# A diffusion step's sums packed into fewer gaps of a dense pipeline, with the boundary product and the next step moved later

## The chip, the cores and the metric

The kernel runs on one core of one Trainium2 chip. The metric is the device time of one execution in microseconds (us); the profile is that of one execution on the same core.

## The reference, cut to what matters

The program is a graph network of four blocks on 50,000 nodes of 256 features with 12,500 edges. What matters here is the last block. It ends in a linear diffusion of six steps (gamma is 0):

```python
x = silu(h @ W_in.T + b_in)
out = term = x
for i in range(1, 7):
    msg = term[src]                                   # gather over edges
    term = (segment_sum(msg, dst) * inv_deg) / i      # per node
    out = out + term
x = layernorm(h + out @ W_out.T + b_out)
```

Nodes that no edge points to have a term of zero: for them the whole network is a chain of dense products and layer norms, row by row.

## The kernel before, in words

The edges are sorted by target and cut into T = 100 tiles of 128 rows of a table. The six steps are computed in reverse (Horner) form, each one reading one of two tables in HBM (`h`, `h2`) and writing the other. One tile of one step, here called **one sum**, is: GpSimd gathers 128 rows by index into `i_messages` (L616, an indirect DMA whose descriptors GpSimd makes), SyncE loads a 128x128 matrix of equal keys `i_equal` (L2726), TensorE multiplies the two into one of four PSUM banks (L2801), VectorE scales it and adds the accumulator into `i_y` (L2838), SyncE stores `i_y` to the other table (L2731).

A step ends with its **boundary**: sums of nodes whose edges cross tiles. SyncE waits until all stores of the step have landed and reads the tiles' end rows back into `i_ends` (L2736), TensorE multiplies them by a triangular matrix (L2797), VectorE adds (L2832), GpSimd scatters the result into the table (`put_bound`, L2769). Only when that scatter has landed may GpSimd gather for the next step.

Beside it, in the same stage (`diffuse`), runs the dense network of the nodes without edges, class `Dense`, 160 units of 256 rows in a software pipeline of 165 **turns**. Each engine's program is written out by hand, in order. A turn has four places called **gaps** at which the engine's part of the diffusion is put in, so there are 660 gaps, 110 for each step. In a turn VectorE runs L709, L711, L714, gap, L866, L907, gap, L889, L891, L881, L882, gap, L873, L875, L900, gap. TensorE runs project (L810), gap, transposes (L674), gap, output product (L828), gap, hidden product (L819), gap. GpSimd runs two gaps, then one power operation `powers` (L926) that serves three layer norms of different units, and two gaps more. `powers` waits for L891 and L882 of the same turn of VectorE. Its result is read by L900 in the same turn of VectorE and by ScalarE (L851, L859), whose L851 must be done before L709 of the next turn.

The function `places` says which sum stands in which gap. Before, sum t of a step that begins at gap g0 stands in gap g0 + t, the boundary in g0 + 105, and the next step begins at g0 + 110. TensorE takes a sum in its gap, VectorE adds it one gap later, SyncE stores it two gaps later. GpSimd makes gathers one gap later, for eight sums ahead, at most two in a gap:

```python
if t == T:
    put_bound(s)
upto_q = min((s + 1) * T if t < T else STEPS * T, s * T + t + AHEAD + 1)
...
for k in range(2):
    if fetched < upto_q:
        get(fetched)
        fetched += 1
```

So at the gap behind the boundary GpSimd scatters and from there makes the next step's first nine gathers, two in a gap. GpSimd's gaps with a number 4k and 4k + 1 lie ahead of `powers` of turn k, 4k + 2 and 4k + 3 behind it. When `diffuse` is done, the stage `output` reads the last table.

Of the kernel before, what the change touches and what calls it, by code (L numbers as in the profile page):

```python
# [16 lines left out]
STEPS = 6  # L17
# [2656 lines left out]

def places(T, gaps):

    at = {}
    for s in range(STEPS):
        g0, g1 = gaps * s // STEPS, gaps * (s + 1) // STEPS
        for t in range(T):  # L2680
            at[g0 + t * (g1 - g0 - 9) // T] = (s, t)
        at[g1 - 5] = (s, T)
    assert len(at) == STEPS * (T + 1)
    return at


def diffuse(net):
# [8 lines left out]
    with Stage(nc) as st:  # L2696
        dn = Dense(net, st.ctx, "n", net.early, Dense.all_units(net) - net.early)
        dn.banks(*st.ps("n_bank", 4))
        banks = st.ps("i_bank", 4)
        acc = st.sb("i_acc", [P, T, D])  # L2700
        M = st.sb("i_messages", [P, D], n=NM)
        EQ = st.sb("i_equal", [P, P], n=NM)
        Y = st.sb("i_y", [P, D], n=NY)
        EF = st.sb("i_ends", [T, 2, D])
        B = st.sb("i_bound", [T, D])
        scale = st.sb("i_scale", [P, STEPS, T])
        acc_in, got, eq_in, stored = st.sem("i_acc_loaded", T // CHUNK), st.sem("i_gathered", NM), st.sem("i_eq_loaded", NM), st.sem("i_stored", NY)
        scale_ready, summed, added, ends_in, scattered, copied = (
            st.sem(f"i_{n}") for n in ("scale_ready", "summed", "added", "ends_loaded", "scattered", "copied"))
        assert T % NM == 0 and T % NY == 0 and T % CHUNK == 0  # L2710
        TURNS = dn.units + 5
        GAPS = TURNS * dn.PIECES
        at = places(T, GAPS)
        nth = lambda s, t: s * (T + 1) + t + 1
        block = st.ctx.enter_context(nc.Block())

        def summed_before(eng, q):
            if q >= NM:
                eng.wait_ge(summed, nth((q - NM) // T, (q - NM) % T))

        @block.sync
        def _(sp):
            def load_eq(q):
                if q < STEPS * T:
                    summed_before(sp, q)
                    sp.dma_start(EQ[q % NM][:], net.eq_tab[q % T, :, :]).then_inc(eq_in[q % NM], 16)  # L2726

            def store(s, t):
                q = s * T + t
                sp.wait_ge(added, nth(s, t))  # L2730
                sp.dma_start(tabs[(s + 1) % 2][t * P:(t + 1) * P, :], Y[q % NY][:]).then_inc(stored[q % NY], 16)  # L2731

            def load_ends(s):
                for b in range(NY):
                    sp.wait_ge(stored[b], 16 * (T // NY) * (s + 1))
                sp.dma_start(EF[:], tabs[(s + 1) % 2][0:R, :].rearrange("(t p) d -> t p d", p=P)[:, 0:2, :]).then_inc(ends_in, 16)  # L2736
            n = itertools.count()

            def gap():
                i = next(n)  # L2740
                if i - 2 in at and at[i - 2][1] < T:
                    store(*at[i - 2])
                    if at[i - 2][1] == T - 1:
                        load_ends(at[i - 2][0])
                if i in at and at[i][1] < T:
                    load_eq(at[i][0] * T + at[i][1] + AHEAD)
            for u in range(2):
                dn.load(sp, 0, u)
            for q in range(AHEAD):
                load_eq(q)  # L2750
            for i in range(TURNS):
                dn.turn_sp(sp, i // 2, i % 2, gap)
            for u in range(2):
                sp.wait_ge(dn.stored[u], 16 * (dn.units // 2))

        @block.gpsimd
        def _(gp):
            def get(q):
                s, t = q // T, q % T
                summed_before(gp, q)  # L2760
                if s:
                    gp.wait_ge(scattered, 16 * s)
                if s == 1:
                    gp.wait_ge(copied, 64)
                gather(net, M[q % NM][:], tabs[s % 2], net.table_row[:, t:t + 1]).then_inc(got[q % NM], 16)

            def put_bound(s):
                gp.wait_ge(added, nth(s, T))
                nc.gpsimd.indirect_dma_start(tabs[(s + 1) % 2], bass.IndirectOffsetOnAxis(net.bound_row[:, 0:1], 0), B[:], None,  # L2769
                                             bounds_check=R - 1, oob_is_err=False).then_inc(scattered, 16)  # L2770
            n, fetched, upto_q = itertools.count(), 0, AHEAD

            def gap():
                nonlocal fetched, upto_q
                i = next(n)
                if i - 1 in at:
                    s, t = at[i - 1]
                    if t == T:
                        put_bound(s)
                    upto_q = min((s + 1) * T if t < T else STEPS * T, s * T + t + AHEAD + 1)  # L2780
# [4 lines that stand above are left out]
            for i in range(TURNS):  # L2785
                dn.turn_gp(gp, i // 2, i % 2, gap)
            gp.wait_ge(scattered, 16 * STEPS)

        @block.tensor
        def _(pe):  # L2790
            def total(s, t):
                q, r = s * T + t, nth(s, t) - 1
                if r >= 4:
                    pe.wait_ge(added, r - 3)
                if t == T:
                    pe.wait_ge(ends_in, 16 * (s + 1))
                    nc.tensor.matmul(banks[r % 4][0:T, 0:D], net.upper[:], EF[:, 0, :], start=True, stop=True).then_inc(summed, 1)  # L2797
                else:
                    pe.wait_ge(eq_in[q % NM], 16 * (q // NM + 1))
                    pe.wait_ge(got[q % NM], 16 * (q // NM + 1))  # L2800
                    nc.tensor.matmul(banks[r % 4][:, 0:D], EQ[q % NM][:], M[q % NM][:], start=True, stop=True).then_inc(summed, 1)  # L2801
            n = itertools.count()

            def gap():
                i = next(n)
                if i in at:
                    total(*at[i])
            for i in range(TURNS):
                dn.turn_pe(pe, i // 2, i % 2, gap)

        @block.scalar
        def _(act):
            for c in range(T // CHUNK):
                act.dma_start(acc[:, c * CHUNK:(c + 1) * CHUNK, :],
                              net.h[c * CHUNK * P:(c + 1) * CHUNK * P, :].rearrange("(t p) d -> p t d", p=P)).then_inc(acc_in[c], 16)
            for c in range(4):
                rows = slice(R + c * (R // 4), R + (c + 1) * (R // 4))
                act.dma_start(net.h2[rows, :], net.h[rows, :]).then_inc(copied, 16)
            for i in range(TURNS):
                dn.turn_act(act, i // 2, i % 2)  # L2820

        @block.vector
        def _(dve):
            V = nc.vector

            def add(s, t):
                q, r = s * T + t, nth(s, t) - 1
                dve.wait_ge(summed, r + 1)
                if t == T:
                    if s:  # L2830
                        dve.wait_ge(scattered, 16 * s)
                    V.tensor_tensor(B[:], banks[r % 4][0:T, 0:D], EF[:, 1, :], ALU.add).then_inc(added, 1)  # L2832
                else:
                    if s == 0 and t % CHUNK == 0:
                        dve.wait_ge(acc_in[t // CHUNK], 16)
                    if q >= NY:
                        dve.wait_ge(stored[q % NY], 16 * (q // NY))
                    V.scalar_tensor_tensor(Y[q % NY][:], banks[r % 4][:, 0:D], scale[:, s, t:t + 1], acc[:, t, :], ALU.mult, ALU.add).then_inc(added, 1)  # L2838
            n = itertools.count()

            def gap():
                i = next(n)
                if i - 1 in at:
                    add(*at[i - 1])
            for s in range(STEPS):
                V.tensor_scalar(scale[:, s, :], net.inv_deg[:], 1.0 / (STEPS - s), None, ALU.mult).then_inc(scale_ready, 1)
            dve.wait_ge(scale_ready, STEPS)
            for i in range(TURNS):
                dn.turn_dve(dve, i // 2, i % 2, gap)
# [218 lines left out]
```

## Time and profile before

| | |
|---|---|
| median of 3 runs | 3917.52 us (3917.25 to 3924.81) |
| the profiled execution | span 3924.5 us; its own time is taken as the 3924.81 us among the runs, so 0.3 us lie around the span |
| stage `diffuse` in the trace | about 2440 to 3725 us |
| TensorE over the span | 83% busy, mean granted clock 0.914 |
| VectorE, GpSimd, ScalarE | 72%, 53%, 48% busy |

Rows of the trace give the start in us from the start of the span, the duration in us, the engine and line, the operation, and in brackets how long the engine had been idle before and what released it. PEld is TensorE's weight load: each fp32 product has several, and in a saturated stretch they stand without holes. DVE is VectorE, POOL GpSimd, ACT ScalarE, PE TensorE.

### The profile page before, as it was taken

Reading aid. Unit: us, or ns where it says so; the run is one execution under the profiler, and the core shown is the slowest. Engines: PE = TensorE matmul, PEld = TensorE weight load, DVE = VectorE, ACT = ScalarE, POOL = GpSimd, SP = SyncE. Lnnn points to the kernel's source line nnn. Section 1 sums busy time; section 2 is a strip of 40 time slices with the busy share of each in tenths; the row PEclk is TensorE's granted clock in tenths of the full one; section 3 lists DMA queues with packets and bytes.
Section 4 is the critical chain, followed back from the end, with each engine's and each line's share of the span. In section 5 each row is a group of like instructions: output and inputs, shape, how many; then the busy total and the mean of one; then the engine's idle time right before and its main releaser. Section 6 shows DMA issues by size and latency. Waiting matters only on the chain. (4 is left out here: it accounts for less than half of the span.)

```text
span 3924.5 us, 56642 instructions
## 1 busy us (share of the span) xinstructions
PE 3261.1 (83%) x14868; PEld 2626.7 (67%) x14868; DVE 2815.4 (72%) x7890; ACT 1882.4 (48%) x5403; POOL 2087.1 (53%) x2120
## 2 busy tenths in 40 slices
PE   5999927688576899477999993599999999999865
PEld 4888715476454566245777772587878787888754
DVE  5676768698587466794666662598989898989733
ACT  3777705466333121142333331366666666666555
POOL 4767500475365666033333322476767676767667
PEclk8999958899799999657999996799999999999998
DMA  5788739443375333183333335886868686878765
GB/s 145 244 244 247 235 95 354 153 134 108 107 211 174 94 88 87 54 247 99 111 116 115 111 110 187 283 252 199 251 201 252 197 251 201 253 208 242 209 210 164
DMA packets 690467, 710.71 MB, mean 181 GB/s; under 512 B 73444, under 2 KB 644190, under 8 KB 689796
## 3 DMA queue, kind: packets, MB, share of 16 engines
q1 hardware_dynamic: 592204, 484.13, 39.8%
q0 software_dynamic: 68288, 181.26, 17.1%
q10 hardware_dynamic: 29660, 41.70, 3.2%
q8 instruction: 126, 2.06, 0.2%
q14 instruction: 189, 1.55, 0.1%
HBM read 427.77 MB, written 296.22 MB: 184 GB/s over the span
## 5 line engine op out<-in xcount | busy, mean ns | idle before, releaser
L616 POOL DMA_INDIRECT s_i_messages<-h,table_row x600 | 614.0, 1023 | 190.4 <-issue 158.3
L2801 PE MATMUL s_i_bank<-s_i_messages,s_i_equal 128*128 128x256 f32 x1200 | 362.5, 386 | 74.3 <-issue 36.6
L926 POOL TENSOR_TENSOR n_powers<-n_powers,neg_half 128x8 f32<-128x8 f32 (+3 forms) x164 | 268.5, 1637 | 229.9 <-DVE n_powers L891 149.4
L851 ACT ACTIVATE n_z<-gamma_bc,n_powers 128x256 f32<-128x256 f32 x320 | 174.8, 593 | 356.5 <-POOL n_powers L926 356.5
L810 PE MATMUL s_n_bank<-w,n_xt 128*128 128x256 f32 x1280 | 306.9, 383 | 22.6 <-DMA n_xt<-in_x_t 22.6
L828 PE MATMUL s_n_bank<-w_out,n_ht 128*128 128x256 f32 x1280 | 311.7, 387 | 5.6 <-ACT n_ht L838 5.3
L2838 DVE SCALAR_TENSOR_TENSOR s_i_y<-s_i_bank,s_i_scale,s_i_acc 128x256 f32<-128x256 f32 x600 | 285.2, 476 | 34.3 <-PE s_i_bank L2801 32.2
L819 PE MATMUL s_n_bank<-n_x3t,w_in 128*128 128x256 f32 x1280 | 303.2, 380 | 0.0
L2801 PEld LDWEIGHTS s_i_bank<-s_i_messages,s_i_equal 128*128 128x128 f32 x1200 | 219.3, 193 | 101.1 <-issue 42.2
L810 PEld LDWEIGHTS s_n_bank<-w,n_xt 128*128 128x128 f32 x1280 | 246.0, 192 | 58.0 <-DMA n_xt<-in_x_t 23.8
L828 PEld LDWEIGHTS s_n_bank<-w_out,n_ht 128*128 128x128 f32 x1280 | 247.3, 195 | 46.2 <-ACT n_ht L838 11.9
L819 PEld LDWEIGHTS s_n_bank<-n_x3t,w_in 128*128 128x128 f32 x1280 | 243.9, 191 | 33.4
L616 POOL DMA_INDIRECT s_a_x<-in_x,index x200 | 197.8, 989 | 97.4 <-issue 96.3
L2101 PE MATMUL s_e_ps_qv<-w_qv,s_e_xt 128*128 128x512 f32 x400 | 189.7, 597 | 0.0
L2116 ACT ACTIVATE s_e_xt<-s_e_ps_t 128x512 f32<-128x512 f32 x100 | 59.7, 597 | 264.3 <-PE s_e_ps_t L2091 264.3
L2405 POOL TENSOR_TENSOR s_g_small<-s_g_small,neg_half 128x2 f32<-128x2 f32 (+1 forms) x51 | 43.7, 857 | 243.2 <-DVE s_g_small L2648 243.2
L2640 DVE SCALAR_TENSOR_TENSOR s_g_y<-s_g_x,real,s_g_bank 128x512 f32<-128x512 f32 x50 | 37.3, 747 | 179.5 <-PE s_g_bank L2496 179.5
L682 ACT ACTIVATE n_squares<-n_u 128x256 f32<-128x256 f32 x320 | 130.2, 408 | 73.2 <-issue 62.5
L2536 ACT ACTIVATE s_g_h<-s_g_hidden,real 128x512 f32<-128x512 f32 x50 | 36.1, 722 | 251.0 <-DVE s_g_hidden L2595 175.8
L900 DVE TENSOR_SCALAR n_x<-n_z,n_small,n_powers 128x256 f32<-128x256 f32 x320 | 118.3, 412 | 50.9 <-POOL n_powers L926 37.2
L695 ACT ACTIVATE n_x3t<-s_n_bank 128x512 f32<-128x512 f32 x160 | 95.4, 596 | 108.6 <-PE s_n_bank L674 103.9
L859 ACT ACTIVATE n_w<-n_w,n_powers 128x256 f32<-128x256 f32 x320 | 142.8, 493 | 9.1 <-POOL n_powers L926 9.1
(444 smaller groups left out, 9169.7 us busy)
## 6 DMA issues: line engine op xcount, KB each, us to landing
h<-s_i_y SPq DMA_DIRECT2D x600, 128.0 KB, 3.9
n_xt<-in_x_t SPq DMA_DIRECT2D x160, 256.0 KB
out<-n_w SPq DMA_DIRECT2D x160, 256.0 KB
s_i_equal<-eq_tab SPq DMA_DIRECT2D x600, 64.0 KB
x<-s_x_rows SPq DMA_DIRECT2D x100, 256.0 KB
out<-s_a_hs SPq DMA_DIRECT2D x100, 128.0 KB
proj_dst<-s_a_hd SPq DMA_DIRECT2D x100, 128.0 KB
h<-s_h_rows SPq DMA_DIRECT2D x50, 256.0 KB, 4.1
```

The lines of the kernel that those rows point to most:

```text
L616: return net.nc.gpsimd.indirect_dma_start(out, None, table, bass.IndirectOffsetOnAxis(index, 0))
L682: sq = self.nc.scalar.activation(self.squares[0][:, g, :], self.U[u][:, g, :], ACT.Square, scale=self.D ** -0.5, accum_out=self.S[u][:, g: ...
L810: mm = self.nc.tensor.matmul(self.pr[:, g * self.D:(g + 1) * self.D], self.XT[u][:, c, g * P:(g + 1) * P], self.net.w12[:, c, :], start=c ...
L819: mm = self.nc.tensor.matmul(self.hd[:, 2 * m * P:2 * (m + 1) * P], self.net.w_in[:, c, m * P:(m + 1) * P], self.X3T[:, c, :], start=c == ...
L828: mm = self.nc.tensor.matmul(self.op[:, g * self.D:(g + 1) * self.D], self.HT[:, m, g * P:(g + 1) * P], self.net.w_out[:, m, :], start=m = ...
L851: sc = self.nc.scalar.activation(self.Z[u][:, g, :], self.net.bc["gamma"][:], ACT.Identity, bias=v[:, 8 + g:9 + g], scale=v[:, 10 + g:11 + g])
L859: nm = self.nc.scalar.activation(self.W[u][:, g, :], self.W[u][:, g, :], ACT.Copy, scale=v[:, 14 + g:15 + g])
L900: nm = self.nc.vector.tensor_scalar(self.X3[u][:, g, :], self.Z[u][:, g, :], s[:, 24 + 2 * g:25 + 2 * g], v[:, 12 + g:13 + g], ALU.subtrac ...
L926: self.nc.gpsimd.tensor_tensor(v[:, 8 + b0:8 + b1], v[:, b0:b1], self.net.neg_half[:, 0:b1 - b0], ALU.pow).then_inc(self.powered, 1)
L2101: mm = nc.tensor.matmul(qvs[b][:, :], XT[b][:, c, :], net.w_qv[:, c, :], start=c == 0, stop=c == C - 1)
L2801: nc.tensor.matmul(banks[r % 4][:, 0:D], EQ[q % NM][:], M[q % NM][:], start=True, stop=True).then_inc(summed, 1)
L2838: V.scalar_tensor_tensor(Y[q % NY][:], banks[r % 4][:, 0:D], scale[:, s, t:t + 1], acc[:, t, :], ALU.mult, ALU.add).then_inc(added, 1)
```

## The change

`places` is given two constants. The 100 sums of a step stand in its first 90 gaps, so every ninth gap from the first (g0, g0 + 9, ..., g0 + 81) holds two sums and the others one. The boundary stands in g0 + 99, and the gaps from g0 + 90 on hold no sum until the next step at g0 + 110. Since a gap may hold several sums, the table of places holds lists and each engine goes through the list. Counted from the last sum, the boundary comes ten gaps later in place of six, and the next step's first sum 21 gaps later in place of eleven.

```diff
 def places(T, gaps):
 
-    at = {}
+    FREE, BEHIND = 20, 9
+    at = {i: [] for i in range(-2, gaps + 2)}
     for s in range(STEPS):
         g0, g1 = gaps * s // STEPS, gaps * (s + 1) // STEPS
         for t in range(T):
-            at[g0 + t * (g1 - g0 - 9) // T] = (s, t)
-        at[g1 - 5] = (s, T)
-    assert len(at) == STEPS * (T + 1)
+            at[g0 + t * (g1 - g0 - FREE) // T].append((s, t))
+        at[g1 - FREE + BEHIND].append((s, T))
+    assert sum(len(v) for v in at.values()) == STEPS * (T + 1)
     return at
...
             def gap():      # SyncE
                 i = next(n)
-                if i - 2 in at and at[i - 2][1] < T:
-                    store(*at[i - 2])
-                    if at[i - 2][1] == T - 1:
-                        load_ends(at[i - 2][0])
-                if i in at and at[i][1] < T:
-                    load_eq(at[i][0] * T + at[i][1] + AHEAD)
+                for s, t in at[i - 2]:
+                    if t < T:
+                        store(s, t)
+                    if t == T - 1:
+                        load_ends(s)
+                for s, t in at[i]:
+                    if t < T:
+                        load_eq(s * T + t + AHEAD)
...
             def gap():      # GpSimd
                 nonlocal fetched, upto_q
                 i = next(n)
-                if i - 1 in at:
-                    s, t = at[i - 1]
+                for s, t in at[i - 1]:
                     if t == T:
                         put_bound(s)
                     upto_q = min((s + 1) * T if t < T else STEPS * T, s * T + t + AHEAD + 1)
...
             def gap():      # TensorE
-                i = next(n)
-                if i in at:
-                    total(*at[i])
+                for s, t in at[next(n)]:
+                    total(s, t)
...
             def gap():      # VectorE
-                i = next(n)
-                if i - 1 in at:
-                    add(*at[i - 1])
+                for s, t in at[next(n) - 1]:
+                    add(s, t)
```

## Rows read from the trace of the kernel before

**Rows 1.** The page, part 1: busy time, share of the span, instructions of each engine.

```profile
PE 3261.1 (83%) x14868; PEld 2626.7 (67%) x14868; DVE 2815.4 (72%) x7890; ACT 1882.4 (48%) x5403; POOL 2087.1 (53%) x2120
```

**Rows 2.** Stretch of 22 turns: us; PE, PEld, DVE, ACT, POOL; clock, DMA share, GB/s.

```profile
2705.71:2867.31 161.60, 161.60 (x794) 142.34 (x793) 153.18 (x419) 106.58 (x330) 123.84 (x107) 1.00 0.87 250
```

**Rows 3.** Timeline of GpSimd, one turn with four gathers.

```profile
2638.84 1.67 POOL L926 TENSOR_TENSOR n_powers<-n_powers,neg_half 128x8 f32<-128x8 f32 x1 [0.47 <-DVE n_powers L891]
2640.70 1.14 POOL L616 DMA_INDIRECT s_i_messages<-h,table_row  x1 [0.19 <-issue]
...
2644.75 0.95 POOL L616 DMA_INDIRECT s_i_messages<-h,table_row  x1 [0.30 <-issue]
2646.18 1.67 POOL L926 TENSOR_TENSOR n_powers<-n_powers,neg_half 128x8 f32<-128x8 f32 x1 [0.49 <-DVE n_powers L891]
```

**Rows 4.** Timeline of TensorE's weight loads in that turn.

```profile
2642.28 0.41 PEld L2801 LDWEIGHTS s_i_bank<-s_i_messages,s_i_equal 128*128 128x128 f32 x2
2642.71 0.57 PEld L674 LDWEIGHTS s_n_bank<-ident,n_x 128*128 128x128 f32 x4
```

**Rows 5.** Timeline of GpSimd, the last turns, project has ended.

```profile
3691.91 1.66 POOL L926 TENSOR_TENSOR n_powers<-n_powers,neg_half 128x8 f32<-128x8 f32 x1 [0.47 <-DVE n_powers L891]
...
3698.82 1.66 POOL L926 TENSOR_TENSOR n_powers<-n_powers,neg_half 128x8 f32<-128x8 f32 x1
...
3705.64 1.03 POOL L926 TENSOR_TENSOR n_powers<-n_powers,neg_half 128x4 f32<-128x4 f32 x1 [3.83 <-DVE n_powers L891]
3710.44 0.70 POOL L926 TENSOR_TENSOR n_powers<-n_powers,neg_half 128x2 f32<-128x2 f32 x1 [3.77 <-DVE n_powers L907]
3714.57 0.70 POOL L926 TENSOR_TENSOR n_powers<-n_powers,neg_half 128x2 f32<-128x2 f32 x1 [3.43 <-DVE n_powers L907]
```

**Rows 6.** Timeline of VectorE: a full turn, then the first of those turns.

```profile
2651.53 0.68 DVE L866 TENSOR_TENSOR n_u<-s_n_bank,c 128x512 f32<-128x512 f32 x1
...
3696.86 0.47 DVE L2838 SCALAR_TENSOR_TENSOR s_i_y<-s_i_bank,s_i_scale,s_i_acc 128x256 f32<-128x256 f32 x1
3697.53 0.17 DVE L907 TENSOR_SCALAR n_powers<-n_small 128x2 f32<-128x2 f32 x1 [0.21 <-ACT n_squares L844]
```

**Rows 7.** Timeline of GpSimd at the first boundary (scatter in gap 106).

```profile
2667.55 1.64 POOL L926 TENSOR_TENSOR n_powers<-n_powers,neg_half 128x8 f32<-128x8 f32 x1 [5.05 <-DVE n_powers L891]
2673.99 1.64 POOL L926 TENSOR_TENSOR n_powers<-n_powers,neg_half 128x8 f32<-128x8 f32 x1 [4.80 <-DVE n_powers L891]
2676.48 1.07 POOL L2769 DMA_INDIRECT h<-s_i_bound,bound_row  x1 [0.85 <-DVE s_i_bound L2832]
2680.45 1.00 POOL L616 DMA_INDIRECT s_i_messages<-h,table_row  x1 [2.90 <-DMA h<-s_i_bound,bound_row]
...
2690.44 1.67 POOL L926 TENSOR_TENSOR n_powers<-n_powers,neg_half 128x8 f32<-128x8 f32 x1
...
2697.55 1.68 POOL L926 TENSOR_TENSOR n_powers<-n_powers,neg_half 128x8 f32<-128x8 f32 x1 [1.51 <-DVE n_powers L891]
...
2705.71 1.67 POOL L926 TENSOR_TENSOR n_powers<-n_powers,neg_half 128x8 f32<-128x8 f32 x1 [0.57 <-DVE n_powers L891]
```

**Rows 8.** Timeline of GpSimd at the second boundary (scatter in gap 216).

```profile
2881.09 1.64 POOL L926 TENSOR_TENSOR n_powers<-n_powers,neg_half 128x8 f32<-128x8 f32 x1 [4.80 <-DVE n_powers L891]
2887.32 1.05 POOL L2769 DMA_INDIRECT h<-s_i_bound,bound_row  x1 [4.60 <-DVE s_i_bound L2832]
2890.94 1.38 POOL L616 DMA_INDIRECT s_i_messages<-h,table_row  x1 [2.56 <-DMA h<-s_i_bound,bound_row]
...
2896.08 1.68 POOL L926 TENSOR_TENSOR n_powers<-n_powers,neg_half 128x8 f32<-128x8 f32 x1
...
2904.22 1.96 POOL L926 TENSOR_TENSOR n_powers<-n_powers,neg_half 128x8 f32<-128x8 f32 x1
```

**Rows 9.** Timeline of VectorE at the first boundary.

```profile
2675.13 0.42 DVE L2832 TENSOR_TENSOR s_i_bound<-s_i_bank,s_i_ends 100x256 f32<-100x256 f32 x1 [0.78 <-PE s_i_bank L2797]
```

**Rows 10.** Waits from 2440 us on: total us, times, longest.

```profile
PE s_i_bank L2797 <- DMA s_i_ends<-h: 16.2, 6, 3.4
```

## The prediction

> **What bounds the kernel now.** I read the page first: TensorE leads with 83% of the span [rows 1], but that is a mean over stages, so the stage `diffuse` has to be read by itself. I took the timeline of GpSimd there and listed the starts of the power operation L926, because there is exactly one in each of the 165 turns: the distance between two starts is the length of a turn. Three kinds appear.
>
> A turn with four sums takes 7.345 us. The 22 turns between 2705.71 and 2867.31 are 161.60 us long, and in that stretch TensorE is busy for every one of them at full clock, with DMA at 0.87 [rows 2]. The weight loads stand without a hole, and one sum holds the array for 0.43 us (2642.28 to 2642.71) [rows 4]. So TensorE sets this length. The others are hardly behind. On GpSimd a turn is 1.67 us of powers, a step of 0.19, and four gathers; the fourth ends at 2645.70 and powers starts at 2646.18, 0.48 later [rows 3]. The chain powers, L900, L709 to L891, powers runs over VectorE with two to three additions in it. Where TensorE has no project any more, it takes 6.91 and 6.82 us from powers to powers [rows 5]. That is without L866, 0.68 us in a full turn [rows 6]. There L907 starts 0.67 after the addition ahead of it, 0.21 of it a wait for ScalarE [rows 6]; with L866 in between it would be about 0.39 + 0.68 = 1.07, so 0.40 more: 7.31 and 7.22, on average 7.27 for the chain in a full turn.
>
> A turn without sums takes 6.44 us (2667.55 to 2673.99) [rows 7]: there the chain with ScalarE's L851 in it sets the length, not TensorE. So a gap without a sum saves only (7.345 - 6.44) / 4 = 0.23 us, though the sum holds TensorE for 0.43.
>
> The boundary turn is the third kind: 16.45 us (2673.99 to 2690.44) [rows 7] or 14.99 us (2881.09 to 2896.08) [rows 8]. The first kind has the scatter behind powers in the turn's program, and eight gathers ahead of the next powers; the second has four. There are three of the first kind (16.45, 16.76, 16.26; mean 16.49) and two of the second (14.99, 14.72; mean 14.86). In both, powers comes the moment the last gather ends, with no idle time noted: the dense pipeline stands still because powers is queued behind the scatter, its landing (first gather 3.97 and 3.62 us after the scatter's start) and the gathers. TensorE's wait for the end rows, 16.2 us in six waits [rows 10], is the eye-catcher of the list of waits, but runs mostly beside this.
>
> **The change part by part.** (a) *Ten double gaps in each step.* TensorE needs 0.43 more for one [rows 4]. GpSimd also makes an extra gather in that turn, ahead of the next powers. Its price shows in the turn behind the second boundary, which has five gathers: 8.14 us from powers to powers, the second powers starting with no wait [rows 8]. Four gathers plus one more at 0.95 + 0.30 from the steady turn say the same: 6.86 + 1.25 = 8.11 [rows 3]. I take 8.12, which is 0.775 more than 7.345. Gathers are strictly paced by the list of places, so they can't be spread over neighbouring turns. The first double of a step has no extra gather (nine are already fetched behind the boundary), the other nine have: 54 x 0.775 = 41.9, and 6 x 0.43 = 2.6. In such a turn TensorE falls idle for 0.35 us, and in the turn behind it may catch up down to the chain's 7.27. Of 22.5 turns of a step with sums 12.5 are single: 75 x 0.075 = 5.6 comes back. Together **+38.9**. Bounds: below, TensorE's price alone, 60 x 0.43 = 25.8; above, no catching up, 44.5.
>
> (b) *Ten more gaps without a sum in each step.* For five steps 12.5 turns x (7.345 - 6.44) = **-11.3**. In the last step they fall on the pipeline's drain, where a turn with four additions took 4.80 and one without 4.13 [rows 5]: **-0.7**.
>
> (c) *The boundaries.* The boundary product now comes ten gaps after the last sum instead of six. SyncE still waits for all stores and reads the end rows two gaps after the last sum; eight gaps of 6.44 / 4 = 1.6 us cover a read for which TensorE waited at most 3.4 us [rows 10]. So TensorE's wait is gone. What is that worth? At the first boundary VectorE idled 0.78 for the product [rows 9], so scatter and powers come 0.78 sooner: 16.49 becomes 15.71. At the second kind the scatter starts 6.23 us after powers, because the addition stands behind L709 to L714, not because of TensorE: nothing is gained, 14.86 stays. The code behind the boundary is the same: scatter, landing, nine gathers, and powers behind them. The gap numbers shift by six, so the kinds swap: three of the second kind (steps 1, 3, 5), two of the first. Before, above 6.44 each: 3 x 10.05 + 2 x 8.42 = 47.0; plus a late turn of 8.16 two turns behind each of the first kind [rows 7], 8.16, 8.19 and 8.46 against 7.345, 2.8 in all; plus the five-gather turn of 8.14 behind each of the second [rows 8], against 6.89 for a turn half with sums, 2.5: 52.3. After: 3 x 8.42 + 2 x 9.27 = 43.8, plus 3 x (8.14 - 6.44) = 5.1; the late turn goes, since the next step's first sum is eleven gaps behind the boundary and not five: 48.9. So **-3.4**. The last boundary has no gathers; there the drain has turns of 4 to 5 us and TensorE's wait is on the path: **-2.7**, a sixth of the 16.2 [rows 10].
>
> (d) *Queues.* SyncE issues the same transfers. Its wait for the stores at the step's end stands ahead of a load two turns early, as before. In a double gap it and GpSimd wait for a sum one gap old, where it was two; a gap is 7.345 / 4 = 1.8 us, so I take zero. DMA carries 5% more per us in the dense part, at 0.87 busy [rows 2]: zero, with the gathers' own time as the bound in the fourth rival.
>
> Sum: 38.9 - 11.3 - 0.7 - 3.4 - 2.7 = **+20.8 us**. The profiled execution took 3924.8 (span 3924.5), 7.3 above the median of the runs; the trace doesn't say why, and the sum is a difference inside `diffuse`, so I add it to the median: 3917.5 + 20.8 = **3938** (3945.6 for an execution like the profiled one).
>
> A rule bears on the extra gather. The trace has gathers of 1.14 us right behind powers, where VectorE runs L900, and of 0.95 elsewhere [rows 3], and one of 1.38 [rows 8]. The Trainium skill, SBUF — State Buffer, section "SBUF: two separate sides", says that while VectorE runs an operation in a two-port mode GpSimd can't write the descriptors of its own DMAs; the section "A bandwidth-pool intuition that's wrong" gives about 0.62 us alone and 3.1 us beside such an operation. By that rule the direction of the trace's 0.19 agrees, its size does not; with the page's 2.5 us more for each of 54 gathers, an estimate, the sum would be about +155, with the trace's own durations it is the +20.8.
>
> **The rivals.** *One: only TensorE's price counts.* GpSimd's 0.48 of slack and the catching up absorb the fifth gather. For it: TensorE is what bounds a single turn [rows 2]. Against: 8.14 with five gathers [rows 8]. Then (a) is 25.8, the sum +7.7: 3925. Chance 0.13.
>
> *Two: TensorE's wait set the boundary after all.* Then the early end rows give back all of the five waits, 13.5 us, in place of the 1.6 in (c): -15.3 there, +8.9 in all: 3926. Against: powers starts the moment the gathers end [rows 7, 8]. Chance 0.06.
>
> *Three, the other side: the standstill at the boundary disappears*, since ten gaps without sums lie behind the product and nothing urgent is queued there. Then all 52.3 of (c) go: 38.9 - 12.0 - 52.3 - 2.7 = -28.1: 3889. It decides from 24.2 us over the five boundaries, 4.8 us at each. For it: half of a 15 us turn is waiting. Against: powers, which the dense part needs in every turn, stays behind scatter and gathers in GpSimd's program, whatever TensorE has to do. Chance 0.08, with partial forms of it.
>
> *Four: the gathers get longer.* DMA is busier and more gathers meet VectorE. If the extra one takes 1.38 [rows 8] in place of 0.95, 54 x 0.43 = +23 more: 3961. Chance 0.05.
>
> **How the numbers follow.** The forecast has 0.68, from 3930 to 3948: the catching up between nothing (+26.4) and all that TensorE needs, the boundaries within 3 us. The range 3922 to 3950 holds it and rivals one and two, some 0.87. What a measurement of this kernel tells from no change is 0.2%, 7.8 us: up to 3925.3. Rival one lies on that edge and goes mostly to no change; so slower 0.79, same 0.12, faster 0.09.
>
> **What would show it.** In the changed kernel's timeline of GpSimd: turns with five gathers, four in nine, of 8.1 us with no idle time ahead of powers, the turns between at 7.27 to 7.35; turns without sums at 6.44, some four a step; boundary turns of 14.9 (three) and 15.7 (two); no wait of L2797 for the end rows; a step of about 213.5 us where it was 209.8. It is wrong if five-gather turns stay near 7.8, if powers no longer starts right behind the gathers at a boundary, or if gathers take over 1.2 us on average.

## The result, and the profile after

The changed kernel takes 3944.42 us (median of 4 runs, 3940.86 to 3949.91) where the kernel before took 3918.65 in the same session. The ratio is 1.0064, with a 95% interval of 1.005 to 1.0079: it is slower, by 25.8 us in the medians. The forecast was +20.8 us, 3938 with a range of 3922 to 3950.

The profiled execution took 3940.86 us with a span of 3939.1. A single trace has a fault for this purpose: the stages ahead of `diffuse`, which no kernel of this study touches, end up to 13 us earlier or later from one execution to the next. So where traces are compared below, the measure is the **stage length**: the time from the first to the last start of the power operation L926, 163 turns. It is 3721.69 - 2454.46 = 1267.2 us before and 3737.18 - 2449.74 = 1287.4 after: +20.2 us. The 95% interval of the ratio answers to 19.6 to 31.0 us, and the 20.2 lies at its lower end. The first of these starts also says where most of the 7.3 us may lie by which the profiled execution of the kernel before was above its median: 2454.46 is the latest among the nine traces of this study (2441.81 to 2454.46).

The stretch of the dense part that answers to [rows 2] is 17 turns long, with nothing but sums in it (us, busy us and count of PE, PEld, DVE, ACT, POOL, then granted clock, DMA share, GB/s):

```profile
2712.59:2841.30 128.71, 128.22 (x623) 111.20 (x623) 119.44 (x330) 82.19 (x255) 104.89 (x92) 1.00 0.88 263
```

A turn is 128.71 / 17 = 7.57 us. TensorE is idle for 0.49 us in the whole stretch and busy for the rest, at full clock: it is still very near its bound, since its own work would need 7.345 + 0.43 x 4/9 = 7.54 us a turn. But it no longer sets the length of the single turn. That shows in the timeline of GpSimd, which is to be read against [rows 3]:

```profile
2719.75 1.66 POOL L926 TENSOR_TENSOR n_powers<-n_powers,neg_half 128x8 f32<-128x8 f32 x1 [0.27 <-DVE n_powers L891]
...
2726.90 0.95 POOL L616 DMA_INDIRECT s_i_messages<-h,table_row  x1 [0.30 <-issue]
2727.87 1.67 POOL L926 TENSOR_TENSOR n_powers<-n_powers,neg_half 128x8 f32<-128x8 f32 x1
2729.73 1.14 POOL L616 DMA_INDIRECT s_i_messages<-h,table_row  x1 [0.19 <-issue]
...
2733.78 0.95 POOL L616 DMA_INDIRECT s_i_messages<-h,table_row  x1 [0.30 <-issue]
2735.01 1.67 POOL L926 TENSOR_TENSOR n_powers<-n_powers,neg_half 128x8 f32<-128x8 f32 x1 [0.28 <-DVE n_powers L891]
```

The first of the two turns has five gathers and takes 8.12 us; powers starts 0.02 us after the last gather, with no idle time noted. The second has four and takes 7.14, where a regular turn of the kernel before takes 7.345. TensorE did not fall idle in the turn with five gathers:

```profile
2719.75:2727.87 8.12, 8.12 (x42) 7.14 (x41) 7.71 (x24) 4.80 (x15) 6.69 (x6) 1.00 0.88 261
2727.87:2735.01 7.14, 7.14 (x36) 6.08 (x35) 6.48 (x19) 4.79 (x15) 5.75 (x6) 1.00 0.82 256
```

The counts (42 matmuls and 36) say that it does more of its work in the long turn and less in the short one: its own turns don't begin and end with powers.

The turns without sums take 6.44 us as before. The boundary answers to [rows 8], scatter ahead of powers and four gathers:

```profile
2659.33 1.64 POOL L926 TENSOR_TENSOR n_powers<-n_powers,neg_half 128x8 f32<-128x8 f32 x1 [4.80 <-DVE n_powers L891]
2665.58 1.07 POOL L2772 DMA_INDIRECT h<-s_i_bound,bound_row  x1 [4.61 <-DVE s_i_bound L2833]
2668.67 1.01 POOL L616 DMA_INDIRECT s_i_messages<-h,table_row  x1 [2.02 <-DMA h<-s_i_bound,bound_row]
...
2673.45 1.68 POOL L926 TENSOR_TENSOR n_powers<-n_powers,neg_half 128x8 f32<-128x8 f32 x1
...
2681.59 1.68 POOL L926 TENSOR_TENSOR n_powers<-n_powers,neg_half 128x8 f32<-128x8 f32 x1
2688.07 1.64 POOL L926 TENSOR_TENSOR n_powers<-n_powers,neg_half 128x8 f32<-128x8 f32 x1 [4.80 <-DVE n_powers L891]
...
2696.24 1.68 POOL L926 TENSOR_TENSOR n_powers<-n_powers,neg_half 128x8 f32<-128x8 f32 x1 [2.77 <-DVE n_powers L891]
...
2704.44 1.67 POOL L926 TENSOR_TENSOR n_powers<-n_powers,neg_half 128x8 f32<-128x8 f32 x1
```

The boundary turn is 14.12 us; there are three such (14.12, 14.19, 14.14). The one behind it has five gathers and takes 8.14. Two turns in a row of 8.17 and 8.20 us follow (2688.07 to 2696.24 to 2704.44), with only three and four gathers in them: these are the first with sums again. The other kind, which answers to [rows 7]:

```profile
2875.84 1.64 POOL L926 TENSOR_TENSOR n_powers<-n_powers,neg_half 128x8 f32<-128x8 f32 x1 [4.80 <-DVE n_powers L891]
2877.69 1.17 POOL L2772 DMA_INDIRECT h<-s_i_bound,bound_row  x1 [0.21 <-issue]
2880.88 1.00 POOL L616 DMA_INDIRECT s_i_messages<-h,table_row  x1 [2.02 <-DMA h<-s_i_bound,bound_row]
...
2891.06 1.68 POOL L926 TENSOR_TENSOR n_powers<-n_powers,neg_half 128x8 f32<-128x8 f32 x1
...
2897.54 1.68 POOL L926 TENSOR_TENSOR n_powers<-n_powers,neg_half 128x8 f32<-128x8 f32 x1 [3.61 <-DVE n_powers L891]
...
2907.13 1.66 POOL L926 TENSOR_TENSOR n_powers<-n_powers,neg_half 128x8 f32<-128x8 f32 x1 [6.71 <-DVE n_powers L891]
```

It takes 15.22 us (both times), and two turns later the first one with sums takes 9.59. TensorE's waits change too. These are the longest in the stage (us, times, longest); the second and third are single waits at its start:

```profile
PE s_n_bank L674 <- DVE n_x L900: 38.6, 8, 8.0
PE s_i_bank L2803 <- DMA s_i_equal<-eq_tab: 36.5, 1, 36.5
PE s_i_bank L2803 <- DVE s_i_y L2839: 32.7, 1, 32.7
PE s_n_bank L828 <- ACT n_ht L838: 17.6, 28, 1.2
```

The wait for the end rows, 16.2 us in [rows 10], is gone; in its place TensorE waits longer for L900, which waits for powers: 38.6 us, where the same list of the kernel before has 19.5.

### The profile page after: what moved, and what is told of

Same layout as the page of the kernel before. It is cut to its first block and busy times, and to the rows that moved or that the text cites. A ratio compares the mean times of both kernels' runs of the same rounds, so it can differ in the third digit from the quotient of the medians.

```text
span 3939.1 us, 56642 instructions
## 1 busy us (share of the span) xinstructions
PE 3261.9 (83%) x14868; PEld 2617.7 (66%) x14868; DVE 2811.3 (71%) x7890; ACT 1879.9 (48%) x5403; POOL 2085.9 (53%) x2120
## 5 line engine op out<-in xcount | busy, mean ns | idle before, releaser
L2803 PE MATMUL s_i_bank<-s_i_messages,s_i_equal 128*128 128x256 f32 x1200 | 351.1, 384 | 72.4 <-DMA s_i_equal<-eq_tab 37.6
L926 POOL TENSOR_TENSOR n_powers<-n_powers,neg_half 128x8 f32<-128x8 f32 (+3 forms) x164 | 267.9, 1633 | 223.7 <-DVE n_powers L891 149.6
L810 PE MATMUL s_n_bank<-w,n_xt 128*128 128x256 f32 x1280 | 306.6, 383 | 21.1 <-DMA n_xt<-in_x_t 21.1
L810 PEld LDWEIGHTS s_n_bank<-w,n_xt 128*128 128x128 f32 x1280 | 246.1, 192 | 55.9 <-DMA n_xt<-in_x_t 21.5
L616 POOL DMA_INDIRECT s_a_x<-in_x,index x200 | 198.0, 990 | 97.7 <-issue 54.4
L900 DVE TENSOR_SCALAR n_x<-n_z,n_small,n_powers 128x256 f32<-128x256 f32 x320 | 120.9, 419 | 73.3 <-POOL n_powers L926 71.4
L616 POOL DMA_INDIRECT s_d_x<-in_x,index x100 | 98.5, 984 | 75.4 <-DVE s_d_y L2035 49.5
```

What stands on the lines that cost most here:

```text
L616: return net.nc.gpsimd.indirect_dma_start(out, None, table, bass.IndirectOffsetOnAxis(index, 0))
L810: mm = self.nc.tensor.matmul(self.pr[:, g * self.D:(g + 1) * self.D], self.XT[u][:, c, g * P:(g + 1) * P], self.net.w12[:, c, :], start=c ...
L900: nm = self.nc.vector.tensor_scalar(self.X3[u][:, g, :], self.Z[u][:, g, :], s[:, 24 + 2 * g:25 + 2 * g], v[:, 12 + g:13 + g], ALU.subtrac ...
L926: self.nc.gpsimd.tensor_tensor(v[:, 8 + b0:8 + b1], v[:, b0:b1], self.net.neg_half[:, 0:b1 - b0], ALU.pow).then_inc(self.powered, 1)
```

## The experiments

All times are medians; each ratio is to the kernel before, run on the same chip in the same session (3918.65 us for the changed kernel, 3918.35 for the four experiments below it, 3918.6 for the last three), with its 95% interval. The stage length is that of the experiment's trace.

| kernel | us | ratio (interval) | stage length |
|---|---|---|---|
| before | 3918.4 | 1 | 1267.2 |
| after | 3944.4 | 1.0064 (1.005, 1.0079) | 1287.4 |
| before, 54 extra gathers | 3947.05 | 1.008 (1.0067, 1.0094) | 1294.7 |
| after, 54 gathers left out | 3928.65 | 1.003 (1.0018, 1.0041) | 1278.6 |
| after, gathers behind powers | 3909.55 | 0.9973 (0.9964, 0.9982) | 1255.7 |
| after, boundary 4 gaps earlier | 3942.09 | 1.0066 (1.0052, 1.0079) | 1293.1 |
| gathers behind powers, FREE = 16 | 3888.93 | 0.9923 (0.991, 0.9936) | 1239.0 |
| the same, places of before | 3921.93 | 1.0012 (1.0003, 1.0021) | 1269.6 |
| the same, FREE = 13 | 3898.83 | 0.9952 (0.9937, 0.9966) | 1247.9 |

**Extra gathers in the kernel before.** This takes GpSimd's part of a double gap by itself: no sum, no addition, no work for TensorE is added.

```diff
+    SCR = st.sb("i_scratch", [P, D])
...
                 for k in range(2):
                     if fetched < upto_q: ...
+                if i - 1 in at and at[i - 1][1] in range(9, 82, 9):
+                    if extra:
+                        gp.wait_ge(scr_in, 16 * extra)
+                    gather(net, SCR[:], net.a["x"], net.table_row[:, t:t + 1]).then_inc(scr_in, 16)
+                    extra += 1
```

> The kernel before with 54 gathers added and nothing else: nine in each step, one behind each of the sums 9, 18, ..., 81, from the input x into a scratch tile that nobody reads. No sum, addition or store is added. Theory (a fifth gather ahead of powers makes the turn 8.1 us, whatever TensorE has to do, and the turns between can give back only down to about 7.15): nine turns become 4 x 8.15 + 5 x 7.15 = 68.4 in place of 66.1, over some 20 turns of each of six steps about +28 us against the kernel before (+22 to +36). Rival (only TensorE's 0.43 us for a sum counts, GpSimd's gathers are covered by its slack): within 4 us of the kernel before.

Measured: +28.7 us in the medians, +27.5 in the stage. The rival is out. GpSimd in this trace:

```profile
2764.57 1.66 POOL L926 TENSOR_TENSOR n_powers<-n_powers,neg_half 128x8 f32<-128x8 f32 x1 [0.28 <-DVE n_powers L891]
...
2770.49 0.96 POOL L616 DMA_INDIRECT s_i_scratch<-in_x,table_row  x1 [0.30 <-issue]
2771.75 0.96 POOL L616 DMA_INDIRECT s_i_messages<-h,table_row  x1 [0.30 <-PE s_i_bank L2809]
2772.73 1.68 POOL L926 TENSOR_TENSOR n_powers<-n_powers,neg_half 128x8 f32<-128x8 f32 x1
...
2779.87 1.67 POOL L926 TENSOR_TENSOR n_powers<-n_powers,neg_half 128x8 f32<-128x8 f32 x1 [0.28 <-DVE n_powers L891]
```

8.16 us with the fifth gather and 7.14 behind it, the same pair as in the changed kernel, though TensorE has nothing more to do. For each of the 54 gathers that is 27.5 / 54 = 0.51 us.

**The second gathers left out of the changed kernel.** The other way round: TensorE, VectorE and SyncE keep the double gaps, GpSimd loses its extra gather.

```diff
+        left_out = lambda q: q % T in range(19, T, 10)
...
-                        get(fetched)
+                        if not left_out(fetched):
+                            get(fetched)
...
-                    pe.wait_ge(got[q % NM], 16 * (q // NM + 1))
+                    if not left_out(q):
+                        pe.wait_ge(got[q % NM], 16 * (q // T + 1 if q % NM == NM - 1 else q // NM + 1))
```

> The changed kernel with 54 gathers left out: in each step those of tiles 19, 29, ..., 99, whose sums then multiply old messages. Sums, additions and stores stay, so double gaps cost TensorE what they did and GpSimd never makes five gathers between two powers in the dense part. The changed kernel's dense part runs at 7.59 us a turn where TensorE alone would need 7.345 + 0.43 x 4/9 = 7.54. Theory with the catching up that the trace of after shows: 7.54 a turn, about -6 us against the changed kernel (-3 to -10). As the prediction priced it (0.345 lost for each double, little given back): about -15. Rival (TensorE alone counts): 0.

Measured: -15.8 us in the medians, outside the -3 to -10 expected and near the -15 of the prediction's price; -8.9 in the stage, inside. The two don't agree well. Of the 14.3 us between the two profiled executions 5.0 lie ahead of the stage, where the kernels are the same (it starts at 2449.74 and 2444.74), and in the same 90 turns of the stretches of sums the changed kernel takes 683.5 us and this one 676.6, so the traces speak for the smaller figure. Both are well off zero and the rival is out, but how much GpSimd adds to TensorE's price is only known as 9 to 16 us. The stretch of the same kind says what TensorE alone makes of it:

```profile
2705.85:2833.74 127.89, 127.89 (x628) 112.65 (x627) 120.25 (x331) 82.24 (x255) 98.92 (x85) 1.00 0.88 258
```

TensorE is busy for all of it again, and 127.89 / 17 = 7.52 us a turn, against the 7.54 worked out. Most double turns take 7.78 and most single ones 7.35.

**Gathers behind powers.** Sums, additions, boundary and stores stay in their places. A list made when the program is built says in which of GpSimd's gaps each gather stands: for a new step from the gap behind the next powers, one in a gap, two where the sum is less than five gaps away.

```diff
+        if s and q % T == 0:
+            i = bound[s - 1] + 1
+            i = i - i % 4 + (6 if i % 4 > 1 else 2)
+        for k in range(2):
+            if q < STEPS * T and q // T == s and (k == 0 or where[q] - i < LEAD) and (q < NM or where[q - NM] < i):
+                plan[i].append(q)
+                q += 1
...
-                for k in range(2):
-                    if fetched < upto_q:
-                        get(fetched)
-                        fetched += 1
+                for q in plan[i]:
+                    get(q)
```

> The changed kernel, but GpSimd makes no gather for the next step until it has run the next powers after the scatter (and the turn's rest), and from there one gather in a gap, two only where the sum is less than five gaps away. Same sums, places, boundary. Theory (at the boundary the dense part stands still because powers is queued behind the scatter's landing and the gathers): boundary turns fall from 14.1 and 15.2 to 7 to 8 us, the five-gather turn behind three of them goes, about -40 us against the changed kernel (-32 to -46), which is below the kernel before. Rival (the standstill comes from the scatter itself, from VectorE's boundary addition or from TensorE): boundary turns above 12 us, at most -8 us.

Measured: 34.9 us less than the changed kernel, 31.7 in the stage, and below the kernel before by 0.27%. The boundary in GpSimd's timeline:

```profile
2663.76 1.64 POOL L926 TENSOR_TENSOR n_powers<-n_powers,neg_half 128x8 f32<-128x8 f32 x1 [4.80 <-DVE n_powers L891]
2670.00 1.07 POOL L2791 DMA_INDIRECT h<-s_i_bound,bound_row  x1 [4.61 <-DVE s_i_bound L2848]
2671.11 1.67 POOL L926 TENSOR_TENSOR n_powers<-n_powers,neg_half 128x8 f32<-128x8 f32 x1
2673.10 1.02 POOL L616 DMA_INDIRECT s_i_messages<-h,table_row  x1 [0.32 <-issue]
...
2677.97 1.68 POOL L926 TENSOR_TENSOR n_powers<-n_powers,neg_half 128x8 f32<-128x8 f32 x1
```

The boundary turn is 7.35 us where it was 14.12, and the first gather finds the scatter landed (0.32 us of idle time in place of 2.02). The boundary turns of this trace are 7.35, 6.46, 7.34, 6.44 and 7.34. So the standstill was the queue in front of powers: the scatter alone, which is still there, costs at most 0.9 us over a turn of 6.44.

The edit does one thing more. Away from the boundaries too the gathers now follow the new list, and in most of a step they run closer ahead of their sums. The 45 turns around the five boundaries take 321.5 us in place of 367.3, which is 45.7 less. The 106 turns in the stretches of sums between them take 820.7 in place of 804.7, which is 16.0 more. From 2640 us on TensorE waits for messages for 9.1 us in 19 waits, where the changed kernel has no such wait; what makes up the rest of the 16.0 is not shown. The order at the boundary is thus worth more than the 31.7 of the whole stage.

**The boundary four gaps earlier**, `FREE, BEHIND = 20, 5`, where TensorE has the short distance of the kernel before to the end rows.

> The changed kernel with BEHIND = 5 in place of 9: the boundary's product stands six gaps after the last sum, as before the change, and the next step's first sum 15 gaps after it. All scatters keep their place ahead of or behind powers. Theory (TensorE's wait for the end rows runs beside GpSimd's queue): the wait of about 3 us comes back at each of six boundaries, and the time grows by at most 0.8 at two of them and 2 to 3 at the last, +2 to +5 us against the changed kernel. Rival (the wait is on the path everywhere): +14 to +17 us.

Measured: -2.3 us in the medians with overlapping intervals, +5.7 in the stage. The wait is back (13.7 us in six, longest 3.3), boundary turns grow by 0.6 to 0.8 at the three of one kind (from 14.12 to 14.75 at the first) and by 1.5 and 1.7 at the two others (from 15.22 to 16.68 and 16.92), where at most 0.8 at two was expected. By either measure it is far from the rival's +14. TensorE's wait for the end rows, which leads the eye in the list, was worth at most a few microseconds.

**How many free gaps are of use.** With the gathers behind powers, `places` was given other constants: `16, 7`, then `10, 5` (which is the list of places of the kernel before), then `13, 6`.

> As the kernel that gathers behind powers, but with FREE = 16 and BEHIND = 7: a step's sums stand in 94 of 110 gaps, six double gaps and not ten, boundary eight gaps after the last sum. Theory: a double gap costs 0.5 to 0.6 us net, a gap given back to single sums costs 0.2, the boundary keeps its turns of 6.5 to 7.5 us: 4 x 0.55 - 4 x 0.2 = 1.4 us a step and fewer five-gather turns, about -12 us (-6 to -16) against the FREE = 20 kernel that gathers behind powers. Rival (with fewer free gaps the next step's gathers come too late, TensorE waits): no gain or a loss.

> FREE = 10, BEHIND = 5, which is the list of places of the kernel before (100 gaps with one sum, boundary six gaps after the last, next step five gaps on), with gathers only behind the next powers and one in a gap where the sum is five or more away. No double gaps. Theory: the standstill of 8 to 10 us at a boundary goes, but the first gather now comes at the first sum's gap and TensorE waits 3 to 6 us for it, with VectorE behind it: -12 to -28 us against the kernel before, so that most of what is to be had comes without any double gap. Rival (the free gaps are what makes the gain; without them the wait for the gathers eats it): within 8 us of the kernel before.

> As e5 with FREE = 13, BEHIND = 6: 97 gaps, three double gaps, boundary seven gaps after the last sum, first sums two to four gaps behind their gathers. Theory: doubles cost 1.6 us a step less than with FREE = 16 and free gaps give back 0.6 less, but TensorE waits for the end rows for up to 2 us and at some steps for the first gathers: within 6 us of FREE = 16, either way.

Measured: FREE = 16 gives 3888.93, 20.6 us below the FREE = 20 kernel (19.6 by the ratios, since the two ran in different sessions; 16.8 in the stage). That is outside the -6 to -16 expected, and 0.77% below the kernel before. It is the fastest of the study. Why it gained more than expected is not shown. FREE = 13 is 9.9 us above it, outside the 6. With the places of before there is no gain at all (1.0012): the expectation of -12 to -28 was wrong and the rival right. TensorE's waits in that trace, from the first full step on:

```profile
PE s_i_bank L2818 <- DMA s_i_messages<-h,table_row: 26.3, 12, 5.8
PE s_i_bank L2814 <- DMA s_i_ends<-h: 14.7, 6, 3.3
```

and in that with FREE = 16:

```profile
PE s_i_bank L2818 <- DMA s_i_messages<-h,table_row: 4.7, 10, 1.7
PE s_i_bank L2814 <- DMA s_i_ends<-h: 0.3, 1, 0.3
```

Without free gaps the late gathers come as a burst again, and a turn with eight of them has 15.9 us:

```profile
2675.17 1.66 POOL L926 TENSOR_TENSOR n_powers<-n_powers,neg_half 128x8 f32<-128x8 f32 x1 [7.17 <-DVE n_powers L891]
...
2691.09 1.68 POOL L926 TENSOR_TENSOR n_powers<-n_powers,neg_half 128x8 f32<-128x8 f32 x1 [4.04 <-DVE n_powers L891]
```

Here powers is not held by the gathers (4.04 us idle ahead of it): VectorE's additions wait for TensorE, which waits for messages, and L891 stands behind them.

## Why the prediction was right, and where its terms were off

The direction held, and so did the mechanism in its two main parts, the double gaps and the standstill at a boundary. The size held partly by luck: (a) came out 5.0 us lower than forecast and (c) 5.5 higher, and the two errors cancel. The five terms against the traces:

| term | forecast | from the trace of after |
|---|---|---|
| (a) double gaps | +38.9 | +33.9 |
| (b) more gaps without a sum | -11.3 | -11.3 |
| (c) boundaries with gathers | -3.4 | about +2.1 |
| drain and last boundary | -3.4 | about -4.7 |
| start of the stage | 0 | +1.3 |
| sum | +20.8 | +21.3 (stage length: +20.2) |

(a) A turn with five gathers takes 8.21 us on average over 49 (8.12 forecast). The turns between take 7.14, not 7.27: the chain from powers to powers is shorter than I had worked out from the last turns of [rows 5, 6]. Five long stretches of sums, 84 turns, take 638.07 us, 7.596 a turn; that is (7.596 - 7.345) x 9/4 = 0.565 for each double gap, 33.9 for 60, where I had 0.65. So more is given back than forecast, and rival one (0.43, TensorE alone) is still not reached. The forecast had TensorE idle for 0.35 us in a turn with five gathers; it was busy for all 8.12 of the one shown above. The two gather experiments show that both engines price a double: 54 fifth gathers alone cost 27.5 us of stage length, and without them 33.9 - 8.9 = 25.0 of the 33.9 are left, 0.42 for each of the 60 doubles, which is TensorE's 0.43. The two prices overlap; they don't add. So rival one had the larger part of (a) right, and GpSimd added the 9 us (up to 16 by the medians) that took it beyond.

(b) Most turns without sums take 6.43 to 6.48 us, as forecast. The -11.3 is the forecast's count of them at this length and no separate measurement; the table leaves 1.1 us of the stage length unexplained.

(c) TensorE's wait for the end rows went, the kinds swapped, powers starts right behind the last gather. The boundary turns are shorter than forecast (14.15 for 14.86, 15.22 for 15.71), mostly because the scatter lands sooner: the first gather waits 2.02 us where it waited 2.90 and 2.56 [rows 7, 8]. Rival two, by which TensorE's wait set the boundary and 13.5 us would come back with it, is out: the wait went and (c) did not shrink. **The step that failed** is "the late turn goes", which stood in (c) at nothing after the change. It doesn't go. After the three boundaries of one kind the turns 25 to 27 and their like take 22.85, 23.08 and 22.86 us where a free, a double and a single turn are 6.44 + 7.78 + 7.345 = 21.57; after the two others the first turn with sums takes 9.59 and 9.14 where one with three additions took 7.11 [rows 7]. That is 4.1 and 4.5 us. In all (c) is 40.7 of standstill, 5.1 of turns with five gathers and 8.6 of these, 54.4, against the 52.3 of before. At the two others a part of it is a lower clock (0.91 over the turn of 9.59), as told below. At the first of the three the clock has no part: TensorE is busy at full clock for both late turns, and its own turns, from project (L810) to project, are 7.96 and 7.34 us long.

```profile
2688.07:2696.24 8.17, 8.17 (x42) 7.19 (x41) 7.29 (x22) 4.89 (x17) 4.62 (x5) 1.00 0.45 116
2696.24:2704.44 8.20, 8.20 (x42) 7.22 (x41) 7.80 (x21) 4.85 (x15) 5.73 (x6) 1.00 0.63 197
```

```profile
2682.86 1.89 PE L810 MATMUL s_n_bank<-w,n_xt 128*128 128x256 f32 x8
...
2690.82 1.89 PE L810 MATMUL s_n_bank<-w,n_xt 128*128 128x256 f32 x8
...
2698.16 1.89 PE L810 MATMUL s_n_bank<-w,n_xt 128*128 128x256 f32 x8
```

So powers comes later and later in TensorE's turn when the sums set in: project starts 2.75 us behind powers in the first of these turns (2688.07 to 2690.82), 1.92 in the second, and 0.69 in the first turn of the long stretch (2712.59 to 2713.28). Why it does, and why it costs this much, is not shown.

(d) The queues cost nothing, as said: gathers have a mean of 1023 ns after and 1025 before, and GpSimd's idle time behind another gather stays at 0.3 us whatever it is put down to. This also takes rival four out. The Trainium skill, SBUF — State Buffer, section "SBUF: two separate sides", would have GpSimd's descriptors wait while VectorE runs an operation in a two-port mode. The trace agrees in sign at most: gathers of 1.14 us right behind powers and of 0.95 elsewhere, and a mean of 0.99 for the 54 gathers added to the kernel before. No run shows in which mode VectorE's operations ran.

Rival three, that the standstill goes with ten free gaps behind the product, was wrong for the reason given: the free gaps are TensorE's and VectorE's, and powers is behind the gathers in GpSimd's program whatever those have to do. But the same free gaps are what makes it possible to take the gathers out of powers' way: with the order changed the standstill went, and without free gaps (10, 5) nothing was gained by it (1.0012).

## What to carry to other kernels

When work is packed closer, ask of each engine what stands ahead of the one short operation on which the others wait. TensorE bounded the dense part and would have priced a double gap at 0.42 us by itself; GpSimd, which looked half idle, had only 0.48 us of slack in a turn, priced its extra gather at 0.51 by itself, and together they cost 0.565. Free slots at a stage's boundary are worth little where a critical operation is queued behind a wait there; put it ahead of the wait first, and then tune how many free slots the round trip needs: here 20 gave -0.27%, 16 gave -0.77%, 13 -0.48%, and 10 no gain.

## What the runs showed of the hardware

Two things were not expected. TensorE's weight loads paused for 8.40 us in a boundary turn with eight gathers, and then the output product's eight took 3.06 us, where the eight of project took 1.70 a little later:

```profile
2893.62 0.72 PEld L674 LDWEIGHTS s_n_bank<-ident,n_x 128*128 128x128 f32 x4 [8.40 <-DVE n_x L900]
2895.43 3.06 PEld L828 LDWEIGHTS s_n_bank<-w_out,n_ht 128*128 128x128 f32 x8 [1.09 <-ACT n_ht L838]
...
2900.68 1.70 PEld L810 LDWEIGHTS s_n_bank<-w,n_xt 128*128 128x128 f32 x8
```

The stretches around it (columns as above, clock third from the right) say that this was the clock:

```profile
2883.00:2893.00 10.00, 2.63 (x13) 1.97 (x11) 1.16 (x3) 0.23 (x1) 7.97 (x9) 0.80 0.32 95
2893.00:2898.60 5.60, 4.29 (x12) 3.26 (x13) 4.07 (x13) 4.56 (x15) 1.99 (x2) 0.50 0.40 117
2900.70:2906.00 5.30, 5.30 (x28) 4.68 (x27) 3.71 (x9) 3.11 (x12) 0.00 (x0) 1.00 0.53 159
```

It is granted half, the 1.2 GHz level, for the turn in which the product has to be made up for, and the full 2.4 GHz only after it. This fits the Trainium skill, TensorE: Matmul & The Clock Gate, Part 1, in that a TensorE left idle is throttled and must be busy again before it is let go. A boundary turn with four gathers shows the same after 7.29 us without a weight load: clock 0.52 in 2676.00 to 2681.10, and again 3.06 us for the output product's eight. The kernel before has it too (0.76 in 2690.44 to 2697.55, 0.79 in 2896.08 to 2904.22), so it is not a price of the change alone.

The other thing is that the scatter's landing was noticed sooner: over the five boundaries the first gathers waited 12.6 us for it before and 10.2 after. The DMA engines were less busy from the scatter's start to the first gather, 0.12 and 0.20 at the two boundaries shown where it was 0.26 and 0.30; that this is the cause is not shown.
